# A two-layer MetaFormer kernel: the first expert layer's weights turned and split inside the first routing, the scales from row norms

## The reference

```
x = x + L0_conv(ln_c(x), ...)          # group gates: sigmoid, group norm, softmax over 8 channels
t = tokens(x); t = t + L0_ffn(ln_t(t), ...)
x = x + L1_conv(ln_c(x), ...)          # 1x1 convolution 256 -> 256 with a bias
t = tokens(x); t = t + L1_ffn(ln_t(t), ...)

L0_ffn: probs = softmax(x @ gate.T); top 2 of 8 experts, weights renormalized
        out = sum_e comb[e] * (silu(x @ w1[e].T) * (x @ w3[e].T)) @ w2[e].T     # hidden 512
L1_ffn: the same routing without renormalization, with biases;
        out = sum_e comb[e] * (silu(x @ w1[e] + b1[e]) @ w2[e] + b2[e])         # hidden 1024
```

## Time and profile before

| | us |
|---|---|
| median of three runs | 1299.41 (1293.02 to 1303.99) |
| the profiled execution | 1302.36 |
| its span, first to last instruction | 1300.5 |
| PE busy | 956.0 (74%) |
| DVE busy | 826.7 (64%) |
| ACT busy | 591.3 (45%) |
| POOL busy | 510.3 (39%) |

### The profile page before, as it was taken

The page is one execution under the profiler, slowest core; times in us unless marked ns, Lnnn a source line. Parts: engine busy times, 40 slices in busy tenths (PEclk is TensorE's granted clock), DMA queues, the critical chain, the costliest instruction groups (busy, mean ns, idle before and its releaser), DMA issues.

```text
span 1300.5 us, 26761 instructions
## 1 busy us (share of the span) xinstructions
PE 956.0 (74%) x7185; PEld 780.9 (60%) x7185; DVE 826.7 (64%) x1934; ACT 591.3 (45%) x1332; POOL 510.3 (39%) x407
## 2 busy tenths in 40 slices
PE   5201086645668899999996388556999999999984
PEld 4100065541566777777774277425888888888873
DVE  6999978779854555555554676693555555555540
ACT  5234443227656565655654023273544444444432
POOL 1385200000105566666664150004555555555650
PEclk8655587555879999999998695557999999999996
DMA  8045321990657888899887703404565664764448
GB/s 260 1 122 163 118 65 33 323 323 1 204 147 180 178 211 205 204 208 208 202 202 192 263 0 133 135 0 102 123 144 83 139 134 77 142 141 73 73 66 266
DMA packets 210852, 189.97 MB, mean 146 GB/s; under 512 B 98992, under 2 KB 184440, under 8 KB 210680
## 3 DMA queue, kind: packets, MB, share of 16 engines
q1 hardware_dynamic: 150632, 108.48, 30.3%
q0 software_dynamic: 27440, 38.97, 17.7%
q10 hardware_dynamic: 32736, 42.02, 10.6%
HBM read 111.22 MB, written 58.79 MB: 131 GB/s over the span
## 4 chain that ended last, share of the span: by engine, by line
PE 35%; DVE 18%; issue 16%; DMA 14%; ACT 8%; ACTq 6%; DVEq 1%; POOL 1%; SPq 1%; POOLq 0%
PE bank L750 13%; PE bank L728 11%; DMA wreg<-in_L_ffn_w_dram 4%; PE bank L661 4%; DMA rows_y<-region 4%; DVE region L1088 4%; PE bank L578 2%; DMA region<-rows_x,region 2%; DVE xt L1102 2%; ACTq L287 2%; ACT region L946 2%; ACT region L950 1%; ACTq L914 1%; PE bank L633 1%; DVE region L1084 1%
## 5 line engine op out<-in xcount | busy, mean ns | idle before, releaser
L728 PE MATMUL bank<-xt,wreg 128*128 x3360 | 383.5, 274 | 18.8 <-DMA xt<-region 13.0
L728 PEld LDWEIGHTS bank<-xt,wreg 128*128 128x128 f16 x3360 | 327.2, 98 | 69.4 <-issue 28.6
L509 POOL DMA_INDIRECT rows_y<-region x140 | 247.6, 1769 | 185.1 <-ACT region L972 93.6
L750 PE MATMUL bank<-wreg,region 128*128 128x256 f16 x2520 | 296.1, 274 | 24.9 <-ACT region L950 18.1
L750 PEld LDWEIGHTS bank<-wreg,region 128*128 128x128 f16 x2520 | 235.6, 98 | 80.6 <-ACT region L950 31.0
L460 POOL DMA_INDIRECT region<-rows_x,region x148 | 149.6, 1011 | 309.8 <-DVE region L1334 154.4
L955 ACT ACTIVATE region<-bank,b_t,wreg 128x256 f32<-128x256 f32 x280 | 135.5, 561 | 20.2 <-PE bank L728 19.3
L972 ACT ACTIVATE region<-region 128x256 f32<-128x256 f32 x70 | 31.7, 500 | 194.7 <-DVE region L1440 189.4
L1435 DVE SCALAR_TENSOR_TENSOR region<-region,wreg 128x512 f16<-128x512 f32 x140 | 105.2, 751 | 5.0
L1432 DVE TENSOR_SCALAR region<-region,wreg 128x512 f16<-128x512 f32 x140 | 70.4, 503 | 50.0 <-ACT region L955 49.9
L946 ACT ACTIVATE region<-bank,fac 128x256 f32<-128x256 f32 x140 | 58.3, 465 | 92.5 <-PE bank L728 55.9
(11 more groups left out here) (241 smaller groups left out, 1207.5 us busy)
## 6 DMA issues: line engine op xcount, KB each, us to landing
wreg<-in_L_ffn_w_dram SPq DMA_DIRECT2D x48, 512.0 KB, 6.9
wreg<-in_L_ffn_w_dram ACTq DMA_DIRECT2D x72, 256.0 KB
split_v<-wreg ACTq DMA_DIRECT2D x36, 512.0 KB
wreg<-in_L_ffn_w_dram SPq DMA_DIRECT2D x64, 256.0 KB, 3.0
wreg<-split_v SPq DMA_DIRECT2D x32, 512.0 KB
rows_x<-region SPq DMA_DIRECT2D x16, 512.0 KB, 4.1
rows_y<-tok SPq DMA_DIRECT2D x16, 512.0 KB, 4.5
tok<-rows_y SPq DMA_DIRECT2D x16, 512.0 KB, 6.0
```

The costliest lines, as they stand in the source:

```text
L509: nc.gpsimd.indirect_dma_start(rows_y[f], bass.IndirectOffsetOnAxis(ap=now[:, b, g_, 1:2], axis=0), y_rows[:, g_, :], None, compute_op=ALU ...
L728: last = pe.matmul(to, block, x_cols[:, bass.ds(b, 1), :, xs_, k, :].rearrange("p j r n -> p (j r) n"), start=(k == 0 and ws_ + xs_ == 0), ...
L750: last = pe.matmul(yb[:, r * C:(r + 1) * C], lhs[:, c, r * P:(r + 1) * P], block, start=first, stop=end, skip_group_check=True)
```

## The change

SP no longer loads 64 pieces for row sums and the first layer's weights for a scan. It loads 56 chunks of 512 KB (24 of the first layer, 32 of the second) through six slots, and ACT squares each, with the row sum of the squares accumulated (`squares`). A square root gives row norms; from these, instead of from largest values, both layers' scales are made. The first layer's scales are ready before the routing. In the routing of layer 0 each unit now turns one expert's weights on PE (24 transposes, into four PSUM banks in rotation, `halves_bank`), ACT writes the high halves (`highs`) and DVE the low ones (`lows0`); the scan is gone, and so is the stretch of turning and splitting behind the routing. The store of the tokens to `rows_y` moves on SP's queue behind the loop. `scales(0)` and `factors(0)` move ahead of the routing, `peaks1` into it, behind unit 1.

```diff
-        sum_in = wreg[:, 30720:32256].rearrange("p (j n) -> p j n", j=3)
+        CHUNKS0, CHUNKS, SLOTS = 3 * E, 7 * E, 6
+        chunk_in = wreg[:, 24576:30720].rearrange("p (j n) -> p j n", j=SLOTS)
...
-        sum_piece = wreg[:, 32256:32256 + 2 * PIECES].rearrange("p (m q) -> p m q", m=2)
+        norms = wreg[:, 32256:32256 + 4 * E].rearrange("p (q m) -> p q m", m=2)
...
+        def load_chunk(eng, n):
+
+            to = chunk_in[:, n % SLOTS]
+            if n < CHUNKS0:
+                e, m = divmod(n, 3)
+                c = (4, 4, KC)[m]
+                ins = eng.dma_start(to.rearrange("p (c d) -> p c d", c=c), (w1, w3, w2)[m][e].rearrange("(c p) d -> p c d", p=P))
+            else:
+                q, m = divmod(n - CHUNKS0, 2)
+                if m == 0:
+                    ins = eng.dma_start(to, v1_rows[q])
+                else:
+                    ins = eng.dma_start(to.rearrange("p (c d) -> p c d", c=4), v2[q // 2, q % 2 * 512:q % 2 * 512 + 512].rearrange("(c p) d -> p c d", p=P))
+            ins.then_inc(chunk_loaded[n % SLOTS], 16)
...
+        def halves_bank(e, q):
+
+            return (zb[2], zb[3], yb, misc)[(6 * e + q) % 4]
...
-            with sp.Fori(0, HB // 2 - 1) as h:
-                for j in range(2):
-                    store_rows(0, 2 * h + j)
-                    sp.wait_ge(peak_ready, 2 * h + j + 1)
-                    load_stage0(2 * h + j + 2, j, scan0_loaded)
-            for j in range(2):
-                store_rows(0, HB - 2 + j)
-                if j:
-                    store_spare(0)
-                sp.wait_ge(peak_ready, E - 1 + j)
-                load_stage0(j, j, stage_loaded)
-            with sp.Fori(1, E // 2) as i:
-                for j in range(2):
-                    sp.wait_ge(w_turned, 6 * (2 * i + j - 1))
-                    load_stage0(2 * i + j, j, stage_loaded)
+            for n in range(CHUNKS):
+                free(sp, summed, n - SLOTS + 1)
+                load_chunk(sp, n)
+            sp.wait_ge(summed, CHUNKS)
+            for e in range(2):
+                load_stage0(e, e, stage_loaded)
+            for e in range(E):
+                store_rows(0, e)
+                if e + 2 < E:
+                    sp.wait_ge(w_turned, 6 * e + 6)
+                    load_stage0(e + 2, e % 2, stage_loaded)
+            for i in range(HB):
+                store_tokens(0, i)
+            store_spare(0)
+
...
+                    pool.wait_ge(peak_ready, 1)
+                    spread_peaks(0)
+                    nc.gpsimd.memset(piece_out[:, 2].rearrange("p m s n -> p (m s n)"), 0.0)
                     pool.wait_ge(peak1_ready, 1)
-                    nc.gpsimd.memset(piece_out[:, 2].rearrange("p m s n -> p (m s n)"), 0.0)
                     spread_peaks(1)
-                    pool.wait_ge(peak_ready, E)
-                    spread_peaks(0)
...
                 def units(i):
                     for j in range(2):
                         norm_turn(2 * f + 1, i, j)
+                    if f == 0:
+                        stage_turns(i, 0, 4)
                     for j in range(2):
                         router(f, i, j)
-
-                pairs(pe, units)
+                    if f == 0:
+                        stage_turns(i, 4, 6)
+
+                if f == 0:
+                    for i in range(HB):
+                        units(i)
+                else:
+                    pairs(pe, units)
 
                 pe.wait_ge(hots_ready[f], 1)
...
+            def stage_turns(e, first, end):
+
+                j = e % 2
+                pe.wait_ge(stage_loaded[j], of_slot(j) + 48 * (e // 2 + 1))
+                for q in range(first, end):
+                    m, k = divmod(q, 2)
+                    to = halves_bank(e, q)
+                    free(pe, w_lo, 6 * e + q - 3)
+                    for c in range(4):
+                        if m < 2:
+                            src = stage0[:, j, m, c * C + k * P:c * C + (k + 1) * P]
+                        else:
+                            at = c % 2 * FH[0] + (2 * k + c // 2) * P
+                            src = stage0[:, j, 2, at:at + P]
+                        last = pe.transpose(to[:, c * P:(c + 1) * P], src, ident[:])
+                    last.then_inc(w_turned, 1)
...
-            edges = []
-            for e in range(E):
-                stage_turns(e // 2, e % 2)
-                edges.append(edge(e))
-            edges.append(edge(E))
-            experts(0, edges)
+            experts(0, [edge(e) for e in range(E + 1)])
...
+            def squares(first, end):
+
+                for n in range(first, min(end, CHUNKS)):
+                    act.wait_ge(chunk_loaded[n % SLOTS], 16 * (n // SLOTS + 1))
+                    to = peak[0][:, n // 3, n % 3:n % 3 + 1] if n < CHUNKS0 else norms[:, (n - CHUNKS0) // 2, n % 2:n % 2 + 1]
+                    act.activation(chunk_in[:, n % SLOTS], chunk_in[:, n % SLOTS], ACT.Square, accum_out=to).then_inc(summed, 1)
+
...
-            sum_pieces(20, 46)
+            squares(12, 30)
             deviation(4)
-            sum_pieces(46, 50)
+            act.activation(peak[0][:].rearrange("p e m -> p (e m)"), peak[0][:].rearrange("p e m -> p (e m)"), ACT.Sqrt
+                           ).then_inc(peak_ready, 1)
+            squares(30, 34)
...
                 mix_gates(i)
-                sum_pieces(50 + 2 * i, min(52 + 2 * i, 2 * PIECES))
+                squares(34 + 3 * i, 37 + 3 * i)
...
+                if f == 0:
+                    act.wait_ge(summed, CHUNKS)
+                    act.activation(norms.rearrange("p q m -> p (q m)"), norms.rearrange("p q m -> p (q m)"), ACT.Sqrt
+                                   ).then_inc(norms_ready, 1)
+                    act.wait_ge(w_scale[0], 1)
+
+                def highs(e):
+
+                    for q in range(6):
+                        act.wait_ge(w_turned, 6 * e + q + 1)
+                        m, k = divmod(q, 2)
+                        to = (w1_s, w3_s)[m][:, e, k, 0, :] if m < 2 else w2_s[:, e, 2 * k:2 * k + 2, 0, :]
+                        src = halves_bank(e, q)[:] if m < 2 else halves_bank(e, q)[:].rearrange("p (c n) -> p c n", c=2)
+                        act.activation(to, src, ACT.Copy, scale=scl[0][:, e, m:m + 1]).then_inc(w_hi, 1)
+
                 def units(i):
...
-                pairs(act, units)
+                if f == 0:
+                    for i in range(HB):
+                        units(i)
+                        highs(i)
+                else:
+                    pairs(act, units)
                 act.wait_ge(exp_in[f], 1)
...
+            edges = [edge(e) for e in range(E + 1)]
+            act.wait_ge(w_scale[1], 1)
...
-                def units(i, i_odd, before=None):
-                    for j in range(2):
-                        norm(s, i, j)
-                    if f == 0:
-                        scan0_peaks(i, i_odd)
-                    if before is not None:
-                        keep_logits(before)
+                def low_rows(i):
...
+                norms_of(0)
+                if f == 0:
+                    for i in range(HB):
+                        low_rows(i)
+                        if i + 1 < HB:
+                            norms_of(i + 1)
+                        lows0(i)
+                        keep_logits(i)
+                        if i == 1:
+                            peaks1()
+                else:
+                    low_rows(0)
+                    with dve.Fori(1, HB) as i:
+                        norms_of(i)
+                        keep_logits(i - 1)
+                        low_rows(i)
+                    keep_logits(HB - 1)
                 for j in range(2):
...
-                dve.wait_ge(summed, 2 * PIECES)
+                dve.wait_ge(norms_ready, 1)
                 dve.tensor_reduce(peak[1][:, :, 2], b1_t[:], AX.X, ALU.max, apply_absolute_value=True)
                 dve.tensor_reduce(peak[1][:, :, 0:2].rearrange("p e m -> p m e"),
-                                  sum_piece.rearrange("p m (e q) -> p m e q", e=E), AX.X, ALU.max).then_inc(peak1_ready, 1)
+                                  norms.rearrange("p (e q) m -> p m e q", e=E), AX.X, ALU.max).then_inc(peak1_ready, 1)
...
-            peaks1()
+            scales(0)
+            factors(0)
             route(0)
-            scales(0)
             scales(1)
+            factors(1)
             edge = lambda e: dve.value_load(bounds[0:1, e:e + 1], min_val=0, max_val=TILES)
-            edges = []
-            for e in range(E):
-                lows0(e)
-                edges.append(edge(e))
-            edges.append(edge(E))
-            dve.wait_ge(w_lo, 6 * E)
-            for f in range(2):
-                factors(f)
+            edges = [edge(e) for e in range(E + 1)]
             experts(0, edges)
```

70 lines of the change are left out of this document (14 added, 56 removed).

## The result

| | before | after |
|---|---|---|
| median of the comparison, us | 1299.09 (1293.02 to 1303.99, 4 runs) | 1260.74 (1257.63 to 1266.44, 4 runs) |
| the profiled execution, us | 1302.36 | 1258.29 |
| its span, us | 1300.5 | 1256.5 |
| mean granted clock of PE | 0.828 | 0.851 |

The ratio is 0.9712, with a 95% interval of 0.9655 to 0.9769. The forecast was 1260 us. A second comparison (e9) gave 1260.60 against 1301.18 us, 0.9697 [0.9665, 0.9729].

The account below looks back on a forecast made before the run. Transfers were taken to pace the routing loop, and a chain of weight loads and PE transposes the hand-over. Terms -38.5 + 0.7 - 4.3 + 0.3 + 1.0 + 0.3 = -40.5 us gave 1260 us, range 1251 to 1280.

Parts of the forecast that it names:

- Term 1: Hand-over from moves_ready to layer 0's first expert matmul: 48.03 us become 9.5, -38.5 us; cold first tile +0.7 us.
- Term 2: Layer 0's routing loop: clock mostly up, DVE pacing at 6.9 us a unit, 60 us in all, -4.3 us.
- prediction's signs of being wrong: Transposes at 0.22 us throughout, DVE waiting for ACT between low halves, or convolution sigmoids beginning later than every 5.84 us.
- Term 3: Ahead of the routing loop: scales(0) and factors(0) added, peaks1 leaves, memset moves into the group norm's chain; +1.0 us.
- Term 4: ACT's squares: 0 us in the convolution's loop, about 0.9 us left; four squares ahead of the softmax's exponential, +0.3 us.
- second hit of the memset: POOL's memset, moved into the group norm's chain, may slow another DVE operation: +1.5 us with it, +0.5 us without.
- The moved store: Store of rows_y behind the routing loop: 15 us, wanted by DVE some 45 us after the loop's end; zero cost.
- The clock at 0.50: Rival in layer 0's routing loop: PE paces at 10.7 us a unit, loop 88 us, total 1288 us; chance 0.09.
- The loads: Rival in layer 0's routing loop: loads pace it, unit stays 8 us, loop 66 us, total 1266 us; chance 0.13.
- The late squares: Rival in the convolution's loop: slow transfers delay squares 0.7 us a unit, at most 6 us, total 1266; chance 0.06.
- Serial turning: Rival in layer 0's routing loop: turning and splitting not overlapped, 18.5 us a unit, total 1348 us; chance 0.04.

Follow-up runs that it names:

- e9: The changed kernel run once more, unaltered, against the kernel before: median 1260.60 us, ratio 0.9697; routing loop 57.6 us.
- e5: Changed kernel with 16 spare transposes in each unit of layer 1's routing: median 1247.43 us, ratio 0.9606 to the kernel before; that loop 38.28 us.
- e6: Changed kernel with 8 spare transposes in each unit of layer 1's routing: median 1242.14 us, ratio 0.9553 to the kernel before; that loop 34.43 us.
- e11: Changed kernel with loads split by matrix and 8 spare transposes per unit of layer 1's routing: median 1240.95 us, ratio 0.9542 to the kernel before.
- e2: Changed kernel with the tokens stored inside the routing loop again: median 1264.35 us, ratio 0.9742 to the kernel before; loop 63.2 us.
- e4: Changed kernel with the first layer's low halves set to zero without reading PSUM: median 1261.04 us, ratio 0.9698 to the kernel before; loop 57.0 us.
- e10: Changed kernel with each weight load split by matrix, issued and awaited separately: median 1252.52 us, ratio 0.9646 to the kernel before; loop 55.3 us.
- e3: Changed kernel with two PSUM banks instead of four for the halves: median 1292.60 us, ratio 0.9951 to the kernel before; loop 87.6 us.
- e7: Changed kernel with the token rows' low halves computed on POOL instead of DVE: median 1273.72 us, ratio 0.9823 to the kernel before; loop 82.3 us.
- e8: Changed kernel with three slots for the squares' chunks instead of six: median 1254.13 us, ratio 0.9672 to the kernel before; 222.2 us ahead of loop.

## Why the prediction was right

- **Term 1, hand-over: 9.5 us forecast, 9.42 measured** (-38.6 against -38.5). Reading it off layer 1's own hand-over the earlier trace rows worked since both have the same gather and transfer, though part of the closeness is luck: in the two chains the gather took 3.98 us here and 3.01 there, the transposing transfer 3.37 and 4.53, and the two differences cancel. Over the profiles of the change this hand-over took 9.4 to 9.7 us. `scales(1)` and `factors(1)` lay beside it: DVE's last of them starts at 328.18 and takes 0.17 us, so it ends 7.5 us before the first matmul. The cold first tile cost 1.1 us, not 0.7: PE comes from a pause there, and the window of 336 to 340 us has a granted clock of 0.50.
- **Term 2, routing loop: 60 us forecast, 58.2 and 57.6 measured.** The step that mattered, the clock goes up because transposes follow one another, was right: 0.91 over the loop, 1.00 from 250 to 265 us. e5 and e6 show it without the rest of the change. The Trainium skill (TensorE: Matmul & The Clock Gate, Part 4: PE-mode transpose) says of transpose mode that the full clock doesn't engage for it; for the transposes of this kernel, which the profile names MATMUL against `ident` without telling their mode, that doesn't hold, though e11's profile shows that the clock doesn't always follow. The reading behind the step was luckier than it looked. It took 16 transposes as enough because of one place, 347.57; at the next pauses of the kernel before, 359.27 and 372.23, the clock stayed low through 16 and the 8 behind them (1.92 us here, 1.04 at full clock):

```profile
359.27 3.68 PE L703 MATMUL bank<-ident,wreg 128*128 128x128 f32 x16 [4.13 <-DMA wreg<-in_L_ffn_w_dram]
362.74 1.92 PE L710 MATMUL bank<-ident,wreg 128*128 128x128 f32 x8
```

DVE's unit was put at 6.9 us and is 6.6 to 6.8 (each low half 0.67 us, exactly); the 0.3 us a unit for shortage of banks was too much, it costs PE 0.97 us but DVE nothing. What the prediction did not see is how near the loads were. It gave them 10 us of time for 6.3, but the load issued at 254.99 was wanted by PE at 262.45, 7.5 us later, and came 1.30 us late; e2, e4 and e10 show the loads nearly level with DVE. Where such a wait is followed by a lower clock it costs more: in e5 PE waited 2.17 us for a load before 265.38, its clock was 0.50 from 270 to 275 us, and this unchanged loop took 61.6 us. Of the prediction's signs of being wrong one showed: DVE waited for ACT between low halves, 1.68 us in the first unit and 0.76 us in the last.
- **Term 3, ahead of the loop: +1.0 forecast,** and Term 4's +0.3; measured -0.7 for both. ACT's square root of the group norm, for which it waits for DVE in both kernels, starts at 153.64 us where the kernel before has 154.90: 1.3 us that no term had. The trace shows where they come from. Before, ACT's table load for the gates' first sigmoid (1.28 us) starts at 52.35, behind its wait for PE, and the sigmoid at 53.65. With the change the first four squares stand ahead of it, the table load lies right behind them at 44.79, within that wait, and the sigmoid starts at 52.02 (e9: 45.13 and 52.36). POOL, which waits for this sigmoid, starts its first product at 52.88 instead of 54.51. Term 4 looked at the squares ahead of the loop only for a delay and missed this. In the convolution's loop 1.0 us of the 1.3 is left (a sigmoid at 184.30 against 185.29), and 0.7 us at the first norm. So what the two terms priced at +1.3 us was +0.6 us. The second hit of the memset, which the term feared, is there, in the timeline of DVE (the memset runs from 154.45 for 1.89 us):

```profile
154.77 0.22 DVE L1075 TENSOR_TENSOR xt<-xt 128x64 f32<-128x64 f32 x1
155.03 1.35 DVE L1076 TENSOR_SCALAR xt<-xt 128x64 f32<-128x64 f32 x1
```

An operation like its neighbours of 0.22 us took 1.35 us, as one did in the earlier trace rows at the memset's old place, where the same operation now takes 0.18 us (216.57). What was lost here was saved there.
- **Term 4, squares: 0 forecast in the loop of the convolution, 0 measured.** Three squares take 3.11 us (pitch 1.04 each), and the sigmoids begin at 178.46, 184.30 and 190.15, each 5.84 or 5.85 us after the last. The rows of ACT in the changed kernel:

```profile
181.19 1.05 ACT L868 ACTIVATE wreg<-wreg 128x1024 f32<-128x1024 f32 x1
...
184.30 0.83 ACT L890 ACTIVATE region<-bank,region 128x256 f32<-128x256 f32 x2
...
190.15 0.82 ACT L890 ACTIVATE region<-bank,region 128x256 f32<-128x256 f32 x2
```

- **The moved store: 0 forecast, and nothing waits for it; but in the loop it was worth 1.6 to 5.5 us (e2)**, which the prediction had only in the transfers' rate.
- **The sum: -40.5 forecast; -44.0 and -46.5 between the spans of the profiled executions (e9's taken against the one profile of before), -38.4 and -40.6 between the medians.** The terms that were summed came to -38.6 + 1.1 - 5.9 - 0.7 = -44.1 us, 3.6 us more than forecast, mostly from the loop and from the 1.3 us that no term had. That the median lies 0.7 us from 1260 is therefore luck in part. The stages agree between both profiles of the change, within 0.6 us each in loop and hand-over. The rest is the spread of single executions, experts above all. Which of the two differences is the better figure stays open within the interval of the ratio, 35 to 44 us by e9's.
- **Rivals.** The clock at 0.50: wrong for this loop, though with more idle time of PE the mean clock was lower (0.66 in e3, 0.72 in e7). Single waits don't decide it: after 2.25 us of waiting for a load in e9 the next 16 transposes still took 1.97 us, after 2.17 us in e5 3.05 us. The loads: half right (above). The late squares: right with three slots (e8, 1.8 to 3.2 us), not with six. Serial turning: right with two banks (e3), and it then takes nearly the whole gain.

## What to carry to other kernels

A stretch that only prepares operands can be hidden in a stage that waits for transfers, if both limits of that stage are written down, the busiest engine and the time at which its loads are issued: here they were so level that over 2 us less of DVE in each unit gave a whole loop only 0.6 us shorter than the shortest unchanged one. Before an experiment's difference in a stage is read as its effect, look how much that stage varies where its code is the same: here by 4 us. Give a chain over three engines enough banks that each is ahead of the next; two instead of four cost 29.4 us, and with them PE's clock fell. Price a moved stage by the same stage elsewhere in the kernel, and check per unit what its engine waits for, since a stage of this kernel that nobody touched takes some 7 us more on one chip than on another (means 346.1 and 353.2 us).
